# Whole transpositions, half spreads and 128 stationary columns in a Swin block

## The reference

```python
xn = ln2d(x) * norm1_g + norm1_b                  # over the 64 channels
w  = window_partition(roll(xn, (-4, -4)), 8)      # 64 windows of 64 tokens
q, k, v = split(w @ in_w.T + in_b, 3)
attn = softmax(q @ k.T / sqrt(8))                 # per window and head
a = (attn @ v) @ out_w.T + out_b
y = x + roll(window_reverse(a @ proj_w.T + proj_b), (4, 4))
z = ln2d(y) * norm2_g + norm2_b
out = y + gelu(z @ fc1_w.T + fc1_b) @ fc2_w.T + fc2_b
```

## Time and profile before

| | |
|---|---|
| runs, us | 86.75, 87.61 (median), 88.52 |
| the profiled execution, us | 87.22 |
| its span, first to last instruction, us | 85.2 |
| mean granted TensorE clock | 0.996 |
| busy, us: PE, DVE, ACT, POOL | 79.6, 64.7, 53.0, 46.8 |
| matmuls, with as many weight loads | 1786 |

### The profile page before, as it was taken

How to read it: one execution, slowest core, us unless ns; L and a number is a source line. 1 busy time by engine, 2 the same in 40 slices (tenths; PEclk the granted TensorE clock), 3 DMA queues, 4 the chain that set the end, 5 groups by cost and what they waited for, 6 DMA issues and landing times.

```text
span 85.2 us, 4265 instructions
## 1 busy us (share of the span) xinstructions
PE 79.6 (93%) x1786; PEld 48.0 (56%) x1786; DVE 64.7 (76%) x208; ACT 53.0 (62%) x89; POOL 46.8 (55%) x58
## 2 busy tenths in 40 slices
PE   5999999889999999799999999999999999999950
PEld 5987757555865767467566637465464423533420
DVE  4999998969789989989789999997943944333260
ACT  0396798879888476588288356664587664725400
POOL 7988829989862972997634675787204041300000
PEclk9999999999999999999999999999999999999998
DMA  0799600121101122101021120000000000032042
GB/s 19 203 331 439 258 31 8 36 66 33 53 32 53 51 84 78 53 1 38 32 100 56 52 64 6 8 0 8 0 8 0 0 0 0 13 118 86 38 162 84
DMA packets 3490, 5.75 MB, mean 67 GB/s; under 512 B 944, under 2 KB 1712, under 8 KB 3344
## 3 DMA queue, kind: packets, MB, share of 16 engines
q1 hardware_dynamic: 2608, 3.08, 10.9%
q10 hardware_dynamic: 864, 2.40, 7.3%
HBM read 2.66 MB, written 1.05 MB: 44 GB/s over the span
## 4 chain that ended last, share of the span: by engine, by line
PE 65%; DVE 18%; issue 8%; DMA 3%; ACT 2%; SPq 1%; DVEq 0%; ACTq 0%
PE ps_s L333 14%; PE ps_u L426 6%; PE ps_u L499 5%; DVE row_max L656 4%; PE ps_m L307 4%; PE ps_s L483 4%; PE ps_t L333 3%; PE ps_t L483 3%; DMA masked<-qk 3%; PE ps_o L467 3%; PE ps_m L483 2%; PE ps_t L409 2%; PE ps_m L297 2%; PE ps_o L499 2%; PE ps_o L442 2%
## 5 line engine op out<-in xcount | busy, mean ns | idle before, releaser
L1058 POOL TENSOR_TENSOR max_x<-max_t,early 128x512 bf16<-128x512 bf16 x14 | 14.7, 1048 | 10.6 <-DVE max_t L669 10.6
L656 DVE TENSOR_REDUCE row_max<-ps_s 128x16 f32<-128x1024 f32 x15 | 18.1, 1209 | 2.5 <-PE ps_s L333 2.2
L915 ACT ACTIVATE probs<-ps_t 128x1024 f32<-128x1024 f32 x13 | 13.3, 1023 | 8.8 <-PE ps_t L409 8.4
L333 PE MATMUL ps_s<-masked,qk 32*64 32x256 f32 x240 | 16.9, 387 | 1.0 <-ACT probs L915 0.4
L333 PE MATMUL ps_t<-masked,qk 32*64 32x256 f32 x224 | 15.5, 387 | 0.0
L1067 POOL TENSOR_TENSOR rstd<-y_var,minus_half 128x4 f32<-128x4 f32 x8 | 8.1, 1010 | 9.9 <-DVE y_var L719 9.8
L333 PEld LDWEIGHTS ps_s<-masked,qk 32*64 32x64 f32 x240 | 8.1, 131 | 5.9 <-issue 2.9
L426 PE MATMUL ps_u<-probs,vz 128*32 128x64 f32 x512 | 10.5, 222 | 0.0
L426 PEld LDWEIGHTS ps_u<-probs,vz 128*32 128x32 f32 x512 | 7.9, 109 | 3.1 <-issue 2.7
L1043 POOL TENSOR_TENSOR rstd<-var,minus_half 128x4 f32<-128x4 f32 x8 | 8.3, 1043 | 1.0 <-DVE var L644 0.4
L282 PE MATMUL ps_t<-zeros 128*128 128x128 f32 x32 | 6.9, 376 | 1.0 <-DVE zeros L817 1.0
(11 more groups left out here) (111 smaller groups left out, 150.6 us busy)
## 6 DMA issues: line engine op xcount, KB each, us to landing
masked<-qk SPq DMA_DIRECT2D x38, 32.0 KB, 2.0
x_ch<-x_ch_d ACTq DMA_DIRECT2D x1, 1024.0 KB, 8.0
out_d<-result SPq DMA_DIRECT2D x3, 256.0 KB, 2.5
x_tok<-x_tok_d ACTq DMA_DIRECT2D x1, 512.0 KB, 6.0
masked<-qk SPq DMA_DIRECT2D x8, 64.0 KB, 2.4
late<-late_d ACTq DMA_DIRECT2D x1, 352.0 KB, 5.2
x_tok<-x_tok_d SPq DMA_DIRECT2D x2, 128.0 KB, 3.4
x_tok<-x_tok_d ACTq DMA_DIRECT2D x1, 256.0 KB, 4.8
```

The lines of the kernel that those rows point to most:

```text
L333: return nc.tensor.matmul(ps[o:o + L, g, n * TOK:(n + 1) * TOK], qk[r:r + RG, b, w, t], masked[r:r + RG, b, :, w, t], start=(n == 0), stop ...
L656: nc.vector.tensor_reduce(row_max[:, w, 0:16], score_bank(k, w)[:].rearrange("q g (h j) -> q (g h) j", j=L), axis=AX.X, op=ALU.max).then_i ...
L915: nc.scalar.activation(probs[:, w, :], scores_t_bank(k, w)[:].rearrange("q g c -> q (g c)"), ACT.Exp).then_inc(probs_done, 1)
L1058: nc.gpsimd.tensor_tensor(max_x[:, k % 2, w, :].rearrange("q (n i) -> q n i", n=16), bf16_high(max_t[:, w, :]).unsqueeze(1).to_broadcast([ ...
```

## The change

x_transpose makes one transposition of 128 x 128 for each block, with the identity whole, in place of four quarter products, and leaves it in the first bank of ps_m; copy_xn reads it from there in plain order. project_qk makes one product for each half w, with the 128 columns of queries and keys stationary. project_v makes one for each block and half, with 128 tokens stationary. y_spread works in strips of 64 columns for all tiles, not for the last two alone. All waits and signals stay.

```diff
--- before.py
+++ after.py
@@ -290,22 +290,16 @@
                 if k >= 1:
                     pe.wait_ge(v_copied, 2 * k)
                 for n in range(BLK):
-                    for u in range(2):
-                        r = slice(L * u, L * u + L)
-                        for w in range(2):
-                            c = n * P + C * w
-                            ins = nc.tensor.matmul(ps_m[C * w:C * w + C, u, n * L:(n + 1) * L],
-                                                   xhat[r, k % 2, c:c + C], ident[r, L * u:L * u + L],
-                                                   start=True, stop=True, tile_position=(L * u, C * w))
+                    ins = nc.tensor.transpose(ps_m[:, 0, n * P:(n + 1) * P],
+                                              xhat[:, k % 2, n * P:(n + 1) * P], ident)
                 ins.then_inc(x_transposed, 1)
 
             def project_qk(k):
                 pe.wait_ge(xn_copied, k + 1)
                 for w in range(2):
                     r = slice(C * w, C * w + C)
-                    for s in range(2):
-                        ins = nc.tensor.matmul(ps_m[C * s:C * s + C, w, 0:TOK], w_qkv[r, C * s:C * s + C],
-                                               xn[r, k % 2, :], start=True, stop=True, tile_position=(C * w, C * s))
+                    ins = nc.tensor.matmul(ps_m[:, w, 0:TOK], w_qkv[r, 0:2 * C], xn[r, k % 2, :],
+                                           start=True, stop=True, tile_position=(C * w, 0))
                 ins.then_inc(qk_projected, 1)
 
             def project_v(k):
@@ -314,11 +308,9 @@
                 for n in range(BLK):
                     for w in range(2):
                         r = slice(C * w, C * w + C)
-                        for u in range(2):
-                            t = slice((2 * n + u) * L, (2 * n + u + 1) * L)
-                            ins = nc.tensor.matmul(ps_m[C * u:C * u + C, w, TOK + n * C:TOK + (n + 1) * C],
-                                                   xn[r, k % 2, t], w_qkv[r, 2 * C:3 * C],
-                                                   start=True, stop=True, tile_position=(C * w, C * u))
+                        ins = nc.tensor.matmul(ps_m[:, w, TOK + n * C:TOK + (n + 1) * C],
+                                               xn[r, k % 2, n * P:(n + 1) * P], w_qkv[r, 2 * C:3 * C],
+                                               start=True, stop=True, tile_position=(C * w, 0))
                 ins.then_inc(v_projected, 1)
 
             def project_qkv(k):
@@ -460,7 +452,7 @@
                     pe.wait_ge(sums_transposed, TILES)
                 else:
                     pe.wait_ge(y_var_done, TILES)
-                cols = 32 if k < TILES - 2 else C
+                cols = C
                 for b in range(BLK):
                     for c in range(0, P, cols):
                         out = spread_bank(k)[c:c + cols].rearrange("q (j b i) -> q j b i", j=4, b=BLK)
@@ -873,9 +865,7 @@
                 act.wait_ge(x_transposed, k + 1)
                 if k >= 2:
                     act.wait_ge(v_projected, k - 1)
-                nc.scalar.activation(xn[:, k % 2, :].rearrange("q (n u i) -> q u n i", n=BLK, u=2),
-                                     ps_m[:, :, 0:P].rearrange("q u (n i) -> q u n i", n=BLK),
-                                     ACT.Copy).then_inc(xn_copied, 1)
+                nc.scalar.activation(xn[:, k % 2, :], ps_m[:, 0, 0:TOK], ACT.Copy).then_inc(xn_copied, 1)
 
             def copy_qk(k):
                 act.wait_ge(v_projected, k + 1)
```

## The result

The kernel after takes 89.13 us in the median of four executions (89.12 to 89.61), the kernel before 87.85 us beside it (86.75 to 88.52). The ratio is 1.0227 with a 95% interval of 1.0162 to 1.0293: slower by about 2.3%. The forecast was 90.1 us in a range of 88.8 to 91.2. Between the two profiled executions it is 89.12 - 87.22 = 1.90 us, where the sum had 2.83. The executions of the kernel before scatter (86.75 to 90.35 us in the 26 beside the first experiments, with a median of 87.92), and the ratios compare its quicker ones. Against that median the kernel after is 1.4% slower.

The account below looks back on a forecast made before the run. PE stretches were taken as bound by streaming time plus entries into forms, fewer instructions alone buying nothing. Added terms by stretch sum to 2.83 us; 87.22 + 2.83 = 90.1 us, in a range of 88.8 to 91.2.

Parts of the forecast that it names:

- Queries and keys: project_qk: still 0.43 when nothing is entered, but from tile 5 on a form must be entered, +0.20 us.
- values: project_v: four rounds, each loading 128 columns at 0.11, take 0.39 us against 0.23, +0.16.
- spread: y_spread in the slots: 0.44 us itself stays, but form 128x64 must now be entered, giving 0.59.
- sum 0.35: y_sum behind the spread in the slots: form 128x32 must be entered again, 0.35 us where it took 0.22.
- shift of tile 4: shift_scores behind tile 4's transposition loses its own cover and must enter its form: +0.12 us.
- the two changes alone: Entering 128x64 for y_spread and 128x32 again for y_sum: 0.15 + 0.13 = 0.28 us in each of five slots.
- Rival (c): Next form's loads are pulled ahead and PE is limited by instructions, so no entry is added: 86.1 us, chance 0.06.
- rival (b): The transposes of x are ordinary products of two passes, 0.64 us each, +1.1 in all: 91.2 us, chance 0.10.
- the cover: From 44.1 to 55.0 us: PE waits of 0.23 and 0.16 pay part of two spreads, leaving +0.17 us.
- the lost 0.5: Scores at 41.53 take 0.71 us where a round takes 0.21; the forecast left this unclaimed 0.5 in.
- Rival (a): Part is absorbed: the lost 0.5 goes, and transposes take the lower bound in three places (-0.3): 89.3 us, chance 0.20.
- the transposition, taken at 0.42: x_transpose: one full-array pass per block, 0.20 + 2 x 0.11 = 0.42 us; +0.19 for tiles 6 and 7.

Follow-up runs that it names:

- e5_two_pass: The kernel after with an ordinary product with the identity in place of the transposing mode for x; 91.11 us.
- e9_spread_back: The kernel after with the old spread (32 stationary columns up to the sixth tile), the two other parts kept; 88.19 us.
- e8_after_more: The kernel after with the first block's score products split into halves of 128 moving columns, 256 matmul and load pairs more; 92.93 us.
- e3_project: The kernel before with the changed project_qk and project_v alone (128 stationary columns); 88.16 us, ratio 1.0108.
- e10_train64: The kernel before with a train of 512 products of zeros, 64 moving columns each, behind its last product; the train takes 27.9 us.

## Why the prediction was right, and too large

Right was the mechanism: forms are paid on entry, the change adds entries on a chain that is PE's, and fewer instructions give no time back in the groups. They do between the groups, and that the sum left out. Its prices held. Queries and keys 0.63 (foreseen 0.63), values 0.39 (0.39), spread 0.59 (0.59), sum 0.35 (0.35), shift of tile 4 0.34 (0.34), and the two changes alone 0.27 (0.28). The loads of values start 0.11 us apart in the last two rounds (37.35, 37.46 and 37.57 in the trace of the kernel after), as foreseen. Rival (c), no price for entries, is out; rival (b), two passes, is out.

By stretches, from the starts of the same groups in the two chains (after against before; 44.11 is an end, with some 0.04 of a matmul's tail):

| stretch to | after | before | measured | foreseen |
|---|---|---|---|---|
| scores at 17.6 | 17.66 | 17.57 | +0.09 | +0.16 |
| scores at 20.0 | 20.10 | 20.00 | +0.01 | +0.14 |
| scores at 34.9, two stretches | 35.41 | 34.91 | +0.40 | +0.59 |
| end of weigh_values, 44.1 | 45.20 | 44.11 | +0.59 | +1.19 |
| scores at 55.0 | 56.33 | 55.00 | +0.24 | +0.17 |
| fc1 | 64.58 | 62.68 | +0.57 | +0.56 |
| last group | 84.00 | 82.10 | 0.00 | +0.02 |

The chain of the kernel after, at the ends of the last stretches:

```profile
45.20 0.43 PE ps_o L434 x8
...
50.52 0.43 PE ps_o L434 x8
50.95 0.43 PE ps_s L325 x4
...
55.90 0.43 PE ps_o L434 x8
56.33 0.43 PE ps_s L325 x4
...
64.58 1.06 PE ps_s L475 x4
```

The scores of 50.95 and 56.33 follow project_out at once, in 0.43, where the earlier trace rows have a wait: the two waits of PE are gone, as foreseen, and with them all of the cover. From 55.0 on the sum is right to 0.01.

What failed is one step: "nothing in the profile claims the lost 0.5, and I leave it in". The kernel after has no such pause; the scores of that place (42.20 to 43.25) take 1.05. That is 0.5 of the 0.9 us by which the sum was too large (2.83 against 1.90), and it makes the stretch to 44.1 come out at 0.59: 1.11 for the groups, of 1.19 foreseen, less the pause of 0.5. The pause was PE's wait for a block of instructions; in the kernel after, with 256 pairs fewer, none of its blocks comes near such a wait. Rival (a) named this, with the instruction stream as its reason, and lay at 89.3 with a chance of 0.20; the forecast's own 90.1 did not come, and the range held because it took rival (a) in.

The second is a term of the wrong size: the transposition, taken at 0.42, measured 0.37. The blocks come in one pass that costs less than a pass of a product of the same columns. That is 0.05 for each of tiles 4, 5 and 7, which lie where PE sets the pace (0.15). For tile 3 it is more: 0.46 in the earlier trace rows becomes 0.38 in the chain of the kernel after, and this takes half of what tile 2's projection delays; the scores behind it wait for DVE's maximum in both kernels, and that starts only 0.09 later (18.82 against 18.73). The rest is in the early stretches: 0.07 less up to the masks, and 0.05 less for L506, which I had at 0.44 and which takes 0.39. The 0.44 was four times 0.11, but the earlier trace rows give 0.53 less 0.20 for the four passes, 0.33 or 0.08 each; the 0.39 lies between.

Still open is what makes one packet land 1.80 us after a block's start and another 2.46. Nor is it shown what spreads the executions of the kernel before over 3.6 us, but the traces, one for each kernel, suggest the same limit. In four kernels every packet past 20 us had landed 1.66 us or more before its block started (the kernel after 2.64, e5_two_pass 2.17, e9_spread_back 1.81, e8_after_more 1.66), and their executions lie within 0.1 to 0.6 us. In eight the closest was 1.25 to 1.48 us, and seven of them spread over 1.7 to 3.6 us; e3_project (1.45) is the exception, with 0.5.

## What to carry to other kernels

Before you merge small products of TensorE into larger ones, read from the chain what stands before and after each: groups of equal work behind different forms give the price of an entry (here 0.12 to 0.20 us), and a merged group that differs in form from both neighbours pays twice. A pause in the midst of a group that waits for nothing is no part of that group's price; don't carry it over into the kernel that you forecast, but give it its own line with both ends. Count instructions as well as columns: a stretch of small products can run out of instructions. To tell such a pause from others, count the engine's instructions up to it; here all of them lie a multiple of 256 apart.

## What was not expected of the hardware

TensorE's instructions come in blocks of 256 (16 KB), one in 3.45 to 3.73 us in the train of e10_train64, and the engine stops for 1.46 to 2.01 us between blocks that it uses up in 1.99; in all traces such a stop ends 1.29 to 1.54 us after a packet's landing. fp32 blocks of 128 x 128 in the transposing mode took one pass each and 0.37 us for two with the entry, where ordinary products took 0.64. A product that streams one column cost 0.06 us in the form of its neighbours and 0.33 in another.
